# Moving the q planes and the m rows of a cross-attention and expert kernel two batches at a time, with four plane buffers and new orders on every queue

## What is computed

```python
q = layernorm(x); k = v = ctx                      # 8 heads of 16 features
i = gate_in @ Wi + bi;  f = gate_in @ Wf + bf      # gate_in = [q, k, v]
csum = cumsum(log_sigmoid(f))
Dt[i, j] = csum[i] - csum[j] + i[j]  for j <= i, else -inf
D = exp(Dt - max_j Dt)
C = (q k^T) * D / 4
h = (C v) / (max(|sum_j C|, exp(-max_j Dt)) + 1e-6)
x = x + groupnorm_per_head(h) * gn_w + gn_b
n = layernorm(x)
x = x + top-2 of 8 experts: sum_e w_e * (silu(n w1_e) w2_e)
      + sigmoid(n g) * ((silu(n A) * (n B)) W)     # the shared expert
```

## Time and profile before

| | |
|---|---|
| median of three runs | 160.41 us |
| the profiled execution | 160.85 us |
| its span, first to last instruction | 158.9 us |
| TensorE busy | 131.2 us (83%) |
| VectorE busy | 128.0 us (81%) |
| ScalarE busy | 77.5 us (49%) |
| GpSimd busy | 75.9 us (48%) |
| mean granted TensorE clock | 0.914 |
| chain that ended last | PE 44%, SyncE's queue 36%, DVE 9%, issue 5%, DMA 3% |

### The profile page before, as it was taken

How to read it: one execution, slowest core, us unless ns; L and a number is a source line. 1 busy time by engine, 2 the same in 40 slices (tenths; PEclk the granted TensorE clock), 3 DMA queues, 4 the chain that set the end, 5 groups by cost and what they waited for, 6 DMA issues and landing times.

```text
span 158.9 us, 4057 instructions
## 1 busy us (share of the span) xinstructions
PE 131.2 (83%) x1347; PEld 93.5 (59%) x1347; DVE 128.0 (81%) x498; ACT 77.5 (49%) x151; POOL 75.9 (48%) x137
## 2 busy tenths in 40 slices
PE   0375655659897789999999899999999999999980
PEld 0254445335565454756555556768887878887860
DVE  4899996528578986596959989999999869988892
ACT  3267993337215213585356595995416342385100
POOL 8436864967787778767399521552551000000000
PEclk9999555555999995999999999999999999999999
DMA  5999911000001000110101000000020020002002
GB/s 143 287 261 245 273 39 25 21 7 9 11 11 28 24 16 12 29 26 21 25 18 28 7 6 0 0 4 0 4 68 0 0 66 6 0 0 68 4 0 66
DMA packets 13780, 7.39 MB, mean 46 GB/s; under 512 B 2192, under 2 KB 13472, under 8 KB 13760
## 3 DMA queue, kind: packets, MB, share of 16 engines
q1 hardware_dynamic: 13584, 6.96, 17.3%
q10 hardware_dynamic: 176, 0.17, 0.6%
HBM read 4.83 MB, written 1.05 MB: 37 GB/s over the span
## 4 chain that ended last, share of the span: by engine, by line
PE 44%; SPq 36%; DVE 9%; issue 5%; DMA 3%; DVEq 0%
PE bank L952 19%; SPq L260 18%; PE bank L934 13%; SPq L265 6%; PE bank L856 4%; DVE xs L1408 3%; PE bank L897 3%; SPq L249 3%; SPq L304 2%; DMA qblk<-qT 2%; PE bank L840 2%; PE bank L868 2%; SPq L246 2%; SPq L270 1%; DMA mr<-pm 1%
## 5 line engine op out<-in xcount | busy, mean ns | idle before, releaser
L952 PEld LDWEIGHTS bank<-w,hh 128*128 128x128 f32 x288 | 36.1, 191 | 5.6 <-issue 2.1
L1408 DVE SCALAR_TENSOR_TENSOR xs<-bank,comb,xs 128x128 f32<-128x128 f32 x128 | 35.9, 343 | 3.3 <-PE bank L952 1.9
L952 PE MATMUL bank<-w,hh 128*128 128x128 f32 x288 | 37.9, 278 | 0.6 <-DVE xs L1408 0.5
L625 ACT ACTIVATE hh<-bank 128x512 f32<-128x512 f32 x36 | 21.4, 595 | 23.6 <-PE bank L934 20.5
L934 PE MATMUL bank<-xnT,w 128*128 128x512 f16 x120 | 31.1, 380 | 0.0
L897 PEld LDWEIGHTS bank<-vx,ct 64*64 64x64 f32 x512 | 16.0, 135 | 5.2 <-issue 4.7
L897 PE MATMUL bank<-vx,ct 64*64 64x17 f32 x512 | 17.4, 208 | 0.2 <-DVE ct L1252 0.2
L934 PEld LDWEIGHTS bank<-xnT,w 128*128 128x128 f16 x120 | 10.8, 98 | 9.1 <-issue 1.9
L856 PE MATMUL bank<-qblk,kT 128*64 128x512 f16 x96 | 15.2, 416 | 0.9 <-DVE ct L1252 0.8
L382 POOL TENSOR_TENSOR kw<-vx,tok 128x128 f32<-128x128 f32 x32 | 11.9, 405 | 6.9 <-PE bank L870 3.5
L409 POOL TENSOR_TENSOR rstd<-ve,const 128x16 f32<-128x16 f32 x4 | 11.6, 2899 | 5.7 <-DVE ve L1311 5.7
(11 more groups left out here) (130 smaller groups left out, 232.3 us busy)
## 6 DMA issues: line engine op xcount, KB each, us to landing
xs<-in_x SPq DMA_DIRECT2D x4, 256.0 KB, 6.3
cx<-in_ctx SPq DMA_DIRECT2D x4, 256.0 KB, 6.6
w<-in_w SPq DMA_DIRECT2D x2, 512.0 KB, 6.8
qblk<-qT SPq DMA_DIRECT2D x64, 16.0 KB, 1.8
out<-xs SPq DMA_DIRECT2D x4, 256.0 KB, 2.3
mr<-in_mr SPq DMA_DIRECT2D x2, 384.0 KB, 6.9
gl<-in_gl SPq DMA_DIRECT2D x1, 384.0 KB, 4.8
mr<-pm SPq DMA_DIRECT2D x24, 4.0 KB
```

The costliest lines, as they stand in the source:

```text
L625: A.activation(hh[:, e], pH[e % 2][:, :], ACT.Silu).then_inc(silu_ready, 1)
L952: ins = pe.matmul(pO[n % 2][:, t * P:(t + 1) * P], hh[:, e, t * P:(t + 1) * P], w2[:, e], start=True, stop=True)
L1408: ins = V.scalar_tensor_tensor(ob[:, a], pO[n % 2][:, t * P:(t + 1) * P], comb[:, f % 2, t, e:e + 1], (ob if e else x2)[:, a], ALU.mult, A ...
```

## The change

- `qblk` has four buffers (`QB`) instead of two, and `qT2` lies by batch, so that one DMA moves the planes of one head for two batches (16 partitions, 2 batches, 2 planes, 256 tokens, 32 KB). A call `q_planes(i, part)` is four of them; there are 32 in all instead of 64. Buffers 0 and 1 are cleared by VectorE, 2 and 3 by GpSimd behind its other clears.
- One DMA moves an m row of two batches: 12 instead of 24. `mr` still has two buffers, so the m rows of batches 2i and 2i + 1 wait for all `pairs` of the two batches before.
- The six loads of expert weights stand behind the first four batches' q planes and the first two batches' g and m rows.
- `xg`, the residual with its bias, is written into `x2` and has no tile of its own.
- The lists of all engines are written in another order. `exp_table()` and `silu_table()` now stand three times each.

The core of the diff; of the new lists only SyncE's stands here in full:

```diff
-        qblk = sb("qblk", [P, 2, 2, H, S], f16)
+        qblk = sb("qblk", [P, QB, 2, H, S], f16)
...
-            def q_planes(b):
-                g = b * TPB // GRP
-                sp.wait_ge(zeros_set, 2)
-                sp.wait_ge(qT_hi, g + 1)
-                sp.wait_ge(qT_lo, g + 1)
-                if b >= 2:
-                    sp.wait_ge(scores_done, TPB * (b - 1))
-                for h in range(H):
+            def q_planes(i, part):
+                if i % 2:
+                    sp.wait_ge(zeros_late, 2)
+                else:
+                    sp.wait_ge(zeros_set, 2)
+                sp.wait_ge(qT_hi, i + 1)
+                sp.wait_ge(qT_lo, i + 1)
+                if i >= 2:
+                    sp.wait_ge(scores_done, TPB * (2 * i - 2))
+                k = 2 * i % QB
+                for h in range(part * H // 2, (part + 1) * H // 2):
                     r = slice(h * HD, (h + 1) * HD)
-                    sp.dma_start(qblk[r, b % 2, :, h, :], qT2[r, :, b * S:(b + 1) * S])\
-                        .then_inc(q_in[b % 2], 16)
-
-            def m_plane(b, p):
-                sp.wait_ge(mplanes_ready, NP * part(b) + p + 1)
-                sp.dma_start(mr[KG + p:KG + p + 1, b % 2], pm[batch_rows(b), p]).then_inc(m_in[b % 2], 16)
-
-            def gm_rows(b):
+                    sp.dma_start(qblk[r, k:k + 2, :, h, :],
+                                 qT2[r, 2 * i:2 * i + 2])\
+                        .then_inc(q_in[i], 16)
+
+            def m_plane(i, p):
+                sp.wait_ge(mplanes_ready, NP * part(2 * i) + p + 1)
+                r = slice(batch_rows(2 * i).start, batch_rows(2 * i + 1).stop)
+                sp.dma_start(mr[KG + p:KG + p + 1, 0:2], pm[r, p]).then_inc(m_in, 16)
+
+            def g_rows(b):
                 sp.wait_ge(outer_in, 48)
                 sp.wait_ge(gplanes_ready, part(b) + 1)
                 sp.dma_start(gl[0:KG, b * S:(b + 1) * S],
                              pg[batch_rows(b)].rearrange("h p s -> h (p s)")).then_inc(g_in[b], 16)
-                if b >= 2:
-                    sp.wait_ge(pairs_done, TPB * (b - 1))
-                m_plane(b, 0)
-                m_plane(b, 1)
-
-            def m_row(b):
-                m_plane(b, 2)
+
+            def m_rows(i):
+                sp.wait_ge(outer_in, 48)
+                if i:
+                    sp.wait_ge(pairs_done, TPB * 2 * i)
+                m_plane(i, 0)
+                m_plane(i, 1)
+
+            def m_row(i):
+                m_plane(i, 2)
+
+            def load_outer():
+                sp.dma_start(gl[0:KR, :].bitcast(u16), gl_d).then_inc(outer_in, 16)
+                for k in range(2):
+                    sp.dma_start(mr[0:KR, k].rearrange("k h s -> k (h s)").bitcast(u16), mr_d).then_inc(outer_in, 16)
+
+            def load_norm():
+                sp.dma_start(gnw[:, :], gnw_d).then_inc(gn_in, 16)
+                sp.dma_start(gnb[:, :], gnb_d).then_inc(gn_in, 16)
+
+            def load_up():
+                sp.dma_start(w1[:, 0:E, :], w1_d.rearrange("e d f -> d e f")).then_inc(w1_in, 16)
+                sp.dma_start(w1[:, E:E + 2, :], gu_d.rearrange("d (g f) -> d g f", g=2)).then_inc(w1_in, 16)
+
+            def load_down():
+                sp.dma_start(wr[:, 0:E], router_d).then_inc(ffn_in, 16)
+                sp.dma_start(wr[:, E:E + 1], gate_d).then_inc(ffn_in, 16)
+                sp.dma_start(w2[:, 0:E, :], w2_d.rearrange("e f d -> f e d")).then_inc(ffn_in, 16)
+                sp.dma_start(w2[:, E, :], down_d).then_inc(ffn_in, 16)
...
-            q_planes(0)
-            q_planes(1)
-            gm_rows(0)
+            load_outer()
+            load_norm()
+            q_planes(0, 0)
+            q_planes(0, 1)
+            q_planes(1, 0)
+            q_planes(1, 1)
+            g_rows(0)
+            g_rows(1)
+            m_rows(0)
             m_row(0)
-            gm_rows(1)
+            load_up()
+            load_down()
+            g_rows(2)
+            g_rows(3)
+            g_rows(4)
+            g_rows(5)
+            g_rows(6)
+            g_rows(7)
+            m_rows(1)
             m_row(1)
-            gm_rows(2)
-            gm_rows(3)
+            q_planes(2, 0)
+            q_planes(2, 1)
+            m_rows(2)
             m_row(2)
+            q_planes(3, 0)
+            q_planes(3, 1)
+            m_rows(3)
             m_row(3)
-            q_planes(2)
-            q_planes(3)
-            gm_rows(4)
-            gm_rows(5)
-            m_row(4)
-            m_row(5)
-            q_planes(4)
-            q_planes(5)
-            q_planes(6)
-            gm_rows(6)
-            q_planes(7)
-            gm_rows(7)
-            m_row(6)
-            m_row(7)
...
-            G.memset(qblk[:, 1].rearrange("p a h s -> p (a h s)").bitcast(f32), 0.0).then_inc(zeros_set, 1)
+            def clear_planes(k):
+                G.memset(qblk[:, k].rearrange("p a h s -> p (a h s)").bitcast(f32), 0.0).then_inc(zeros_late, 1)
+
...
+            clear_planes(2)
+            clear_planes(3)
             root(0)
...
+            for k in range(2):
+                V.memset(qblk[:, k].rearrange("p a h s -> p (a h s)").bitcast(f32), 0.0).then_inc(zeros_set, 1)
             stats(0)
```

More of the change, by code:

```diff
@@ L24 @@
 LOGS = 4
+QB = 4
 W1P = 5
@@ L1006, in _ @@
             inter(4)
+            intra(3, 1)
             pairs(4, 0)
-            intra(3, 1)
-            xn_turn(0)
-            pairs(4, 1)
-            pairs(5, 0)
-            states(5)
-            pairs(5, 1)
-            scores(4, 0)
-            hidden(0, 0)
+            pairs(4, 1)
+            scores(4, 0)
+            states(5)
+            pairs(5, 0)
+            pairs(5, 1)
+            xn_turn(0)
+            scores(4, 1)
             inter(5)
-            scores(4, 1)
             intra(4, 0)
+            scores(5, 0)
@@ L1019, in _ @@
             intra(4, 1)
-            hidden(0, 1)
-            scores(5, 0)
-            states(6)
-            hidden(0, 2)
             scores(5, 1)
             intra(5, 0)
+            states(6)
+            intra(5, 1)
+            pairs(6, 0)
+            hidden(0, 0)
+            inter(6)
+            pairs(6, 1)
+            pairs(7, 0)
+            logits(0)
+            hidden(0, 1)
+            pairs(7, 1)
+            scores(6, 0)
+            states(7)
+            scores(6, 1)
+            intra(6, 0)
@@ L1026, in _ @@
+            inter(7)
+            scores(7, 0)
+            intra(6, 1)
+            scores(7, 1)
+            down(0, 0)
+            intra(7, 0)
+            intra(7, 1)
+            hidden(0, 2)
+            down(0, 1)
             hidden(0, 3)
-            intra(5, 1)
+            down(0, 2)
             hidden(0, 4)
             hidden(0, 5)
-            inter(6)
+            down(0, 3)
             hidden(0, 6)
+            down(0, 4)
             hidden(0, 7)
-            logits(0)
+            down(0, 5)
@@ L1034, in _ @@
             hidden(0, 8)
             xn_turn(1)
+            down(0, 6)
             hidden(0, 9)
-            states(7)
-            down(0, 0)
             logits(1)
-            inter(7)
-            pairs(6, 0)
-            pairs(6, 1)
             hidden(1, 0)
-            scores(6, 0)
+            down(0, 7)
             hidden(1, 1)
-            down(0, 1)
-            scores(6, 1)
-            intra(6, 0)
-            intra(6, 1)
+            hidden(1, 2)
             xn_turn(2)
-            pairs(7, 0)
@@ L1052, in _ @@
-            pairs(7, 1)
-            hidden(1, 2)
             hidden(1, 3)
-            down(0, 2)
-            logits(2)
-            scores(7, 0)
-            down(0, 3)
-            down(0, 4)
-            intra(7, 0)
-            scores(7, 1)
-            hidden(1, 4)
-            hidden(1, 5)
-            down(0, 5)
-            intra(7, 1)
-            hidden(1, 6)
-            down(0, 6)
-            hidden(1, 7)
-            down(0, 7)
-            hidden(1, 8)
+            hidden(1, 4)
@@ L1071, in _ @@
             down(0, 8)
             down(1, 0)
+            logits(2)
+            hidden(1, 5)
+            down(1, 1)
+            hidden(1, 6)
+            xn_turn(3)
+            down(1, 2)
+            hidden(1, 7)
+            hidden(1, 8)
+            down(1, 3)
             hidden(1, 9)
-            down(1, 1)
-            down(1, 2)
+            down(1, 4)
             hidden(2, 0)
-            down(1, 3)
+            down(1, 5)
+            logits(3)
+            down(1, 6)
             hidden(2, 1)
+            down(1, 7)
@@ L1098, in _ @@
+            hidden(2, 8)
+            down(2, 4)
+            down(2, 5)
+            hidden(2, 9)
+            down(2, 6)
+            down(2, 7)
             hidden(3, 0)
-            down(2, 4)
             hidden(3, 1)
-            down(2, 5)
+            down(2, 8)
+            down(3, 0)
             hidden(3, 2)
-            down(2, 6)
+            down(3, 1)
             hidden(3, 3)
+            down(3, 2)
             hidden(3, 4)
```

(21 more changed lines are left out.)

412 lines of the change are left out of this document (185 added, 227 removed).

## The result

The changed kernel took 162.22 us, the median of 20 runs (161.11 to 168.56), beside 159.96 for the kernel before (20 runs, 158.24 to 162.84). The ratio is 1.0147, with a 95% interval of 1.0109 to 1.0184. I had forecast 155.3 us, and 151.3 to 160.3 as the range: the time lies outside it, on the other side of no change. Executions of one kernel fall into a fast and a slower group, and ratios here compare only the fast ones. The profiled execution took 161.11 us, its span is 159.3, and the mean granted clock 0.907.

The account below looks back on a forecast made before the run. SyncE's queue, busy with issuing, was taken to bound until 75 us, then TensorE. Start 30.0 + work 116.6 + idle 4.5 + tail 4.2 - clock 1.7 + VectorE 0.5 = 154.1 span; median 155.6, said 155.3, range 151.3 to 160.3.

Parts of the forecast that it names:

- The start: Start of attention: first pairs at 30.0 us instead of 33.66, a gain of 3.7.
- The price of a doubled DMA: SyncE's q DMAs: one issue stays at 0.59 us, at most 1.19; landing stays at 1.8 to 2.0.
- rival 3: SyncE's q DMAs: a doubled one costs double, first pairs at 39.5, 165 us in all; chance 0.09.
- The weights: Expert weights issued at 29 to 32.5 us: waits of w1_high() and split_router() cost 0 to 1.7, taken as 0.
- The m rows: Later SyncE queue: m rows without second buffer need 3.1 us, hidden by 1.6; without that cover 3 times up to 3.1.
- rival 4: SyncE's queue isn't freed: m rows without a second buffer bind, 9 us, 164 us in all; chance 0.04.
- `intra(3, 1)` ended: Attention on TensorE: this call ends near 61 us, against 66 before.
- the clock: TensorE's low clock of 59.6 to 63.6 us, costing about 1.7, doesn't return; bounds 0 and 1.7 gained.
- rival 2: Attention: waits for VectorE of 10 us instead of 4.5 and the clock drop stays, about 161 us; chance 0.16.
- VectorE beside GpSimd: Up to 88 us: VectorE instructions are slower while GpSimd runs, 0.5 us added, bounds 0 and 2.5.
- no clock near 0.57 behind 40 us: Sign that the forecast holds: TensorE's granted clock shows no such low stretch after 40 us.
- the three that were to show me wrong: 32 KB issue over 0.9 us; VectorE or ScalarE waiting on weights over 2 us; TensorE below 85% busy, 40 to 88.

Follow-up runs that it names:

- e2_weigh_first: Changed kernel with weigh_scores(4, 1) ahead of token_stats(2) and refine_root(3) in VectorE's list; 155.91 us, ratio 0.9796 to the kernel before.
- e5_w1_late: Changed kernel with GpSimd's residual(3) ahead of w1_low(1) to w1_low(4) instead of behind; 155.31 us, ratio 0.969 to the kernel before.
- e8_both: Changed kernel with the edits of e2_weigh_first and e5_w1_late together; four executions of 155.06, 157.27, 162.59 and 162.87 us, no ratio.
- e3_queue_only: Kernel before with only the new SyncE list and buffers, old lists elsewhere but for two moved calls; 159.7 us, ratio 0.9961 to the kernel before.
- e9_products: e5_w1_late plus four thrown-away two-operand products on GpSimd where w1_low(1) to w1_low(4) had stood; 162.67 us, ratio 1.0104 to the kernel before.
- the clears: e5_w1_late plus four clears of an unused tile on GpSimd where w1_low(1) to w1_low(4) had stood; 161.72 us, ratio 1.011 to the kernel before.
- e1_filled: Changed kernel with seven more thrown-away matmuls on TensorE ahead of scores(5, 0); 156.45 us, ratio 0.9776 to the kernel before.

## Why the prediction was wrong

**Right.** The start: 29.91 (30.0 forecast; its own terms, 28.4 and 1.77, give 30.2). The price of a doubled DMA: 0.58 to 0.60, issued every 0.71, landing 2.0; rival 3 is out. What the prediction has from the Trainium skill, "DMA: Bandwidth & Descriptors" (Anatomy of one DMA), is said there of DMAs that GpSimd issues; for SyncE's these rows decide, and they came out the same way. The weights: `w1_high()` and `split_router()` did not wait. The m rows: SyncE waited for pairs 9.5 us in all, TensorE for m rows never after the first; rival 4 is out. `intra(3, 1)` ended at 59.8 (61). The tail from `intra(7, 1)` to TensorE's end took 61.5 us, and I had (154.1 - 4.2) - 88 = 61.9. With the collision gone, e2_weigh_first has its `intra(7, 1)` at 86.6 (88) and takes 155.9, e5_w1_late 155.3. The terms hold one by one in e2_weigh_first, from 29.9 to TensorE's end at 148.6: 113.5 us of TensorE's work (114.9), 5.2 idle (4.5 and the 0.5 for VectorE), 4.0 behind (4.2). That e5_w1_late hits 155.3 exactly is luck, as its low clock in 40 to 43 us is in no term.

**The step that failed** is the clock: "I expect it not to return, as attention no longer stops for planes; bounds 0 and 1.7 gained". It came back for 13 us, from about 68.5 to 82, and cost over 5: from 29.9 on TensorE was busy 119.8 us, and I had 114.9. The bounds had no loss in them, although rival 2 kept the drop and charged the 1.7 as not gained.

Its reason, too, was a wrong reading. I had put the idle time of 40 to 59.6, and so the drop behind it, down to SyncE's planes. TensorE's own waits in the kernel before, from 33.6 us on (who, for whom, in total, times, longest), and the call at the drop:

```profile
PE bank L840 <- DMA mr<-pm: 3.4, 1, 3.4
PE bank L868 <- DVE ti L1272: 1.5, 2, 0.9
PE bank L856 <- DVE ct L1252: 0.8, 1, 0.8
59.75 1.61 PE L868 MATMUL bank<-kw,cx 128*128 128x408 f32 x2 [0.67 <-DVE ti L1272]
```

The only wait for a DMA is the one that ends at 33.66, ahead of the first pairs. All others of any size are for VectorE, and so is the one just ahead of the drop. Attention had not stopped for planes before either, so taking the planes out of its way was no reason for the clock to stay up; and what I held against rival 2 ("those waits were SyncE's") was wrong. The blocks of DMAs on the chain of waits were not what TensorE stood for.

The drop of before lasted 4 us; I took that length as its price, and the one after lasted three times as long. What decides this is open. The waits of 0.60 (48.9 us, changed kernel) and 0.71 us (e2_weigh_first) had no low clock behind them; those of 0.67 (before), 1.16 (e8_both), 2.45 (e3_queue_only) and 1.59 us (changed kernel) had one, for some 4, 3.5, 3 and 13 us.

**What set it off** was in my text too, and mis-sized: "VectorE beside GpSimd +0.5, bounds 0 and 2.5". The total was within the bounds (2.0 us at this place), but I spread it evenly, as VectorE time. It fell on one chain with no slack, ahead of `weigh_scores(4, 1)`. The earlier trace rows had shown the pairing. What I did not do was to lay GpSimd's new list beside VectorE's new list and ask which call stands behind the colliding ones. The clock then made of the hole's 1.6 us the 6.7 by which the span of e2_weigh_first is shorter.

Rival 2 named the outcome, 161, by other sums: 5.5 us more waiting, spread, and 1.7 for the clock, of which its sum books only 1 (with 1.7 it says 162.5). Measured after 29.9: 4.0 us of TensorE's idle time ahead of 93.6 and 1.4 behind (5.4, I had 4.5), and the low clock for the rest. Of the signs that I had named, "no clock near 0.57 behind 40 us" failed; none of the three that were to show me wrong came (TensorE was busy 44.4 of the 48 us from 40 to 88). The DMA share "5 to 11%" is 5 to 10% in the earlier trace rows.

The Trainium skill, "TensorE: Matmul & The Clock Gate" (HAM oscillation), held against me: the low clock followed the hole, and filling the hole with useless work kept it away. The waits of its example are longer ones, for DMAs; here 1.59 us were followed by the low clock. Nor does it cover the low clock at 40 us in e5_w1_late, ahead of which TensorE did not wait. It had been named in the prediction as a rule that speaks against the change, and given no term of its own. The Trainium skill, "SBUF — State Buffer" (Who interferes with whom), has VectorE and GpSimd blocking each other for an instruction's length. The products agree (0.71 to 0.78 beside GpSimd's 0.70); the 3.10 us across several GpSimd instructions and the clears (2.5 to 2.6 across four) are longer than that.

## What to carry to other kernels

When lists of engines are written anew, look for rows without a gap on GpSimd, and at what small VectorE instructions beside them hold up; such a row, moved behind one call, was worth over 4% here (ratios 1.0147 and 0.969 to the kernel before). Ask of an idle engine what it itself waits for, before putting its idle time down to whoever stands on the chain of waits. Give a hole on TensorE two terms, one for itself and one, with a loss among its bounds, for the clock behind it: here 1.6 us and over 5. One call moved saved both; matmuls thrown away saved the second. Parts of a change that may only pay together (here queue and lists) should be costed together and tried apart: alone one gave nothing that can be measured and the other cost 12%.

## What I had not expected of the hardware

- A clock row can differ from the durations. In e1_filled the granted clock reads 1.00 from 30 to 36 us, yet there:

```profile
31.33 1.49 PE L880 MATMUL bank<-qblk,kT 128*64 128x512 f16 x6 [0.35 <-ACT dd L604]
```

  is the duration of the low clock, as in the changed kernel at 71.25; at the full one it is 0.84. Of the changed kernel's 20 executions three have a mean clock of 0.907 or 0.908 and took 161.1 to 161.3 us, nine have 0.951 to 0.955 and took 161.3 to 162.6: the higher mean is not the faster. A low stretch at the start that the record lacks would explain it (in the profiled one it is some 14 us at half clock, 0.04 of the mean), but only the 0.907 has a trace. Where row and duration disagree, the duration decides.
- An instruction of 128x16 on VectorE took 3.10 us beside eight of GpSimd's without a gap (e3_queue_only), and the same one 0.18 in e5_w1_late and e9_products.
